# Drive products of the scan moved to GpSimd in the woven rows, with the first half's decays in PSUM

## The chip, the cores and the metric

One Trainium2 chip; the kernel runs on one core of it, in one launch. The metric is the device time of one execution in microseconds (us). The kernel before takes 1443.02 us (median of 3 runs, 1440.24 to 1448.51).

## What is computed

Four batch rows of 512 tokens with 128 channels pass four blocks, each followed by a residual sum and a layer norm: sparse latent attention, a mixture of 16 small experts, a Mamba layer, and a top-1 mixture of 8 experts. The change is in the Mamba layer, whose state recurrence is

```python
dA = jnp.exp(jnp.einsum('bld,dn->lbdn', delta, A))
dBu = jnp.einsum('bld,bln,bld->lbdn', delta, Bp, u)
def step(state, inp):
    a, b, c = inp
    state = a * state + b
    y = jnp.einsum('bdn,bn->bd', state, c)
    return (state, y)
```

with 256 inner channels d and 16 states n.

## The kernel before

Each batch row goes through `attention(b)` and then `rest(b)` (experts, Mamba layer, top-1 experts). The two are woven: while one row's attention runs, the row before goes through its rest. Every engine has its own queue of instructions, written by Python generators; a `yield` ends a phase, and `weave` takes one phase of the attention and then one of the rest, on each engine alike. What an engine has in its queue it executes in that order; between engines there are semaphores. So there are four rests: those of rows 0 and 1 stand in a hardware loop (`Fori`), whose semaphore thresholds are computed in registers, that of row 2 stands behind the loop with constant thresholds, woven too, and that of row 3 runs alone. Below they are the two loop rows, the third row and the last row.

The scan stage takes 16 steps, one for each state n; the 512 tokens lie on the free axis, 128 of the 256 channels on the partitions, and the two channel halves are j = 0 and 1. A step n consists of

- the decays, `exp(A_n * delta)`, 128x512 for each half, by ScalarE (ACT, L1201). In a woven row they go to SBUF (`dA`, a part of `big`, two buffers by n % 2), in the last row to PSUM banks 0 to 3;
- the drive product `dBu = DU * B_n`, 128x1024 for both halves, by VectorE (DVE, `drive`, L1713) in a woven row, by GpSimd (POOL, L1294) in the last row. It has two buffers as well;
- the two scans, `tensor_tensor_scan`, by VectorE (L1725);
- the readout product `hC = state * C_n` by VectorE (L1738, in the last row L1736), into XP and CV in turn;
- the sum over the states, by TensorE (PE, L866), in PSUM banks 5 and 6.

In a woven row VectorE issues the drive product of step n + 1 behind the scans of step n and ahead of its readout product, and the first one ahead of step 0. ScalarE issues the decays of steps 0 and 1 in the first phase and then, in each phase, those one step ahead. Rows B_n and C_n are spread over the partitions by DMAs of the SP queue, four steps ahead (tile `BC`). GpSimd has nothing to do in the woven scan stages.

Attention's instructions lie between the steps, among them one-hot builds of the picked key columns (VectorE, L1499, from float16 to bfloat16, SBUF to SBUF; TensorE L708 picks with them), copies of the picks (ScalarE L1068), top-k (MAX8, FIND_INDEX8, MATCH_REPLACE8), index scores (L1407, L1411), rotations (L1396), local maxima (L1460, with their negation `nml` L1465) and the spreading of the queries QBD (ScalarE L1052).

## Time and profile before

| | us |
|---|---|
| median of 3 runs | 1443.02 |
| the profiled execution | 1442.37 |
| its span, first to last instruction | 1440.6 |
| busy: TensorE (matmul) | 908.0 |
| busy: VectorE | 990.2 |
| busy: ScalarE | 584.6 |
| busy: GpSimd | 83.8 |
| scan stages of the loop rows, from the first scan | 107.4 each |
| scan stage of the third row | 102.5 |
| scan stage of the last row | about 60 |

The busy shares are means over stages with different limits; what a change is worth is read from the stage that it touches. In the rows below, a row of the instructions in order of time has the start, the duration, the engine, the line of the kernel, the operation, the tile written and those read, and the shapes; xN says how many instructions are merged in it. What stands in brackets is the engine's idle time in front and what ended it.

### The profile page before, as it was taken

What the parts mean: (1) busy time and instruction counts of PE and PEld (TensorE: products, weight loads), DVE (VectorE), ACT (ScalarE), POOL (GpSimd) and SP (SyncE); (2) the same over time, 40 slices, a digit from 0 to 9 for tenths busy, and PEclk for the clock granted to TensorE, in tenths of its full rate; (3) what the DMA queues carried; (4) which work ended last, traced back from release to release, by engine and by line L of the source; (5) the groups of instructions that cost most, each with busy time, mean ns of one, the idle gap of its engine ahead of it and who ended that gap; (6) DMA issues with size and microseconds to landing.
All of it is one profiled execution on the core that took longest, in us unless ns stands there. A gap on an engine that the chain in (4) does not pass through costs nothing.

```text
span 1440.6 us, 30987 instructions
## 1 busy us (share of the span) xinstructions
PE 908.0 (63%) x11808; PEld 541.5 (38%) x11808; DVE 990.2 (69%) x2294; ACT 584.6 (41%) x1278; POOL 83.8 (6%) x56
## 2 busy tenths in 40 slices
PE   4556656778456576677656568577757567562555
PEld 2334534445224253444323335344424235240122
DVE  4355553566799986655789986746789987344985
ACT  2423332566552332376544232366643331444320
POOL 0000000010000000011000000011000000030630
PEclk9566868597769789688769779598757879575895
DMA  4110110311232210221123310031033310302320
GB/s 140 30 39 10 32 39 10 68 35 35 70 82 76 57 31 18 51 50 38 62 62 79 82 30 7 13 88 39 15 92 96 79 34 10 67 0 60 110 66 8
DMA packets 84840, 72.38 MB, mean 50 GB/s; under 512 B 24528, under 2 KB 63440, under 8 KB 84496
## 3 DMA queue, kind: packets, MB, share of 16 engines
q1 hardware_dynamic: 84688, 70.34, 19.2%
q8 instruction: 97, 1.59, 0.5%
q14 instruction: 55, 0.45, 0.1%
HBM read 66.51 MB, written 3.80 MB: 49 GB/s over the span
## 4 chain that ended last, share of the span: by engine, by line
DVE 37%; PE 26%; issue 16%; ACT 13%; DMA 4%; SPq 3%; DVEq 1%; ACTq 0%; POOL 0%; POOLq 0%
DVE SG L1725 5%; PE bank L708 4%; PE bank L536 3%; DVE Y L1818 3%; PE bank L740 3%; SPq L473 2%; DVE XP L1738 2%; ACT relu_s L1016 2%; DVE CV L1738 2%; PE bank L866 2%; DVE bank L1725 1%; ACT QBD L1052 1%; DVE ml L1460 1%; PE bank L816 1%; DVE big L1700 1%
## 5 line engine op out<-in xcount | busy, mean ns | idle before, releaser
L708 PE MATMUL bank<-onehot,tparts 128*32 128x256 bf16 x3840 | 134.9, 300 | 46.0 <-DVE onehot L1499 45.1
L708 PEld LDWEIGHTS bank<-onehot,tparts 128*32 128x32 bf16 x3840 | 107.2, 105 | 82.6 <-DVE onehot L1499 44.4
L866 PE MATMUL bank<-XP,CO 128*128 128x512 f32 x128 | 84.6, 796 | 63.4 <-DVE XP L1736 33.8
L1725 DVE TENSOR_TENSOR_SCAN SG<-big 128x512 f32<-128x512 f32 x96 | 111.8, 1206 | 5.3 <-DVE score L1429 1.8
L1201 ACT ACTIVATE big<-DEL,Aneg 128x512 f32<-128x512 f32 x96 | 63.8, 715 | 109.1 <-DVE SG L1725 103.1
L1016 ACT ACTIVATE relu_s<-bank,nml 128x192 f32<-128x192 f32 (+1 forms) x128 | 53.0, 426 | 113.2 <-DVE nml L1465 113.2
L866 PE MATMUL bank<-CV,CO 128*128 128x512 f32 x128 | 74.1, 707 | 38.4 <-DVE CV L1738 26.3
L1499 DVE TENSOR_SCALAR onehot<-ib,CO 128x1024 bf16<-128x1024 f16 x160 | 69.8, 478 | 16.2 <-PE bank L708 11.0
L740 PE MATMUL bank<-GT,QBD 128*32 128x32 f32 x3072 | 55.8, 206 | 39.1 <-DVE G L1508 27.9
L1460 DVE TENSOR_REDUCE ml<-bank 128x2 f32<-128x384 f32 (+1 forms) x64 | 33.8, 569 | 67.1 <-PE bank L643 36.5
L536 PE MATMUL bank<-CO,relu_s 128*128 128x128 f32 (+2 forms) x256 | 46.2, 341 | 47.8 <-ACT relu_s L1016 47.8
L740 PEld LDWEIGHTS bank<-GT,QBD 128*32 128x32 f32 x3072 | 53.5, 117 | 46.2 <-issue 46.1
L1068 ACT ACTIVATE GT<-bank 128x256 f32<-128x256 f32 x64 | 24.5, 383 | 109.0 <-PE bank L708 108.8
L866 PEld LDWEIGHTS bank<-XP,CO 128*128 128x128 f32 x128 | 28.0, 242 | 102.8 <-issue 48.6
L1506 DVE TENSOR_TENSOR GT<-bank,rank_turn 128x512 f32<-128x512 f32 x64 | 44.0, 688 | 29.4 <-ACT GT L1068 28.7
L536 PEld LDWEIGHTS bank<-CO,relu_s 128*128 128x128 f32 (+2 forms) x256 | 36.4, 162 | 59.2 <-issue 57.7
L1713 DVE TENSOR_TENSOR big<-DU,BC 128x1024 f32<-128x1024 f32 x48 | 57.7, 1202 | 0.3
L1052 ACT ACTIVATE QBD<-QT 32x768 f32<-32x768 f32 x64 | 53.7, 839 | 7.3 <-DVE QT L1489 6.8
L816 PE MATMUL bank<-XRT,W 128*128 128x512 f32 (+1 forms) x72 | 52.7, 823 | 4.9 <-DVE U L1646 4.9
L536 PE MATMUL bank<-CO,QB 128*128 128x128 f32 x80 | 19.5, 391 | 56.2 <-DVE QB L1401 51.1
L866 PEld LDWEIGHTS bank<-CV,CO 128*128 128x128 f32 x128 | 25.0, 217 | 78.4 <-DVE CV L1738 36.9
L1818 DVE SCALAR_TENSOR_TENSOR Y<-bank,gate,Y 128x128 f32<-128x128 f32 x128 | 44.9, 351 | 13.1 <-PE bank L889 7.4
(313 smaller groups left out, 1999.4 us busy)
## 6 DMA issues: line engine op xcount, KB each, us to landing
BC<-bc_rows SPq DMA_DIRECT2D x128, 256.0 KB, 4.4
ib<-idx_rows SPq DMA_DIRECT2D x64, 256.0 KB, 4.1
big<-comb_rows SPq DMA_DIRECT2D x8, 1024.0 KB, 10.1
rows_bounce<-RO SPq DMA_DIRECT2D x256, 8.5 KB
W<-w SPq DMA_DIRECT2D x1, 2818.0 KB, 15.1
RB<-rows_bounce SPq DMA_DIRECT2D x16, 136.0 KB, 2.1
X<-x SPq DMA_DIRECT2D x4, 256.0 KB, 3.0
out<-CV SPq DMA_DIRECT2D x4, 256.0 KB, 2.3
```

Of the source, the lines that this page charges most:

```text
L536: return pe.transpose(o, i_, ident[0:k, 0:k])
L708: m = mm(bank[2 + c % 2][32 * bb:32 * bb + 32, 256 * kind:256 * kind + 256], tparts[:, kt, part, 32 * kind:32 * kind + 32], onehot[:, n % ...
L740: m = mm(bank[0][32 * a:32 * a + 32, 32 * xx:32 * xx + 32], QBD[:, kind, t, :, :].rearrange("p b h -> p (b h)"), GT[:, kind, t, :], start= ...
L816: mm(bank[k0][0:rows, :], wg, XRT[:, :], start=True, stop=True).then_inc(ga_ps.sem, ga_ps.up())
L866: mm(bank[5 + j][:, :], ident, hC[(n - 1) % 2][:, j, :], start=(n == 1), stop=(n == DS)).then_inc(ysum.sem, ysum.up())
L1016: m = A(PL[:, hh, c0:224], sc, ACT.Exp, scale=SCALE, bias=nml[:, h:h + 1], accum_out=ll[:, h:h + 1])
L1052: m = A(QBD[32 * bb:32 * bb + 32, :, :, bb, :], QT[32 * bb:32 * bb + 32, :, :, :], ACT.Copy)
L1201: A(decay, DEL[:, j, :], ACT.Exp, scale=Aneg[:, j, n:n + 1]).then_inc(dA_ok.sem, dA_ok.up())
L1499: TS(onehot[:, n % 4, :], ib[:, c, :], co("pos")[:, kt:kt + 1], None, ALU.is_equal).then_inc(oh_ok.sem, oh_ok.up())
L1713: TT(dBu[:, n % 2, :, :], DU[:, :, :], BC[:, n % ROWS_AHEAD, 0:1, :].to_broadcast([P, 2, L]), ALU.mult).then_inc(dBu_ok.sem, dBu_ok.up())
L1725: m = dve.tensor_tensor_scan(state, decay, dBu[:, n % 2, j, :], 0.0, ALU.mult, ALU.add)
L1818: STT(out=Y2[:, i, :], in0=bank[TOP1_BANKS[i][k]][:, e * P:(e + 1) * P], scalar=gate[:, i, 4 * k + e:4 * k + e + 1], in1=Y2[:, i, :], op0= ...
```

## The change

The drive products of the woven rows move from VectorE to GpSimd. GpSimd's product n waits for the readout of step n - 2 (in the last row, as before, for its scans). The decays of half j = 0 of a woven row go to PSUM bank 7, which has one buffer: ScalarE writes them after the first scan of the step before, for which the new signal `half_ok` stands, and issues j = 1 ahead of j = 0. ScalarE's decays of step n now stand in the phase of step n; they were one phase ahead.

```diff
--- before.py
+++ after.py
@@ -225,6 +225,13 @@
         ez, eu = big[:, 0, :, :], big[:, 1, :, :]
         BC = sb("BC", [P, ROWS_AHEAD, 2, L])
         hs = SG
+
+        def decay_of(n, j, alone):
+
+            if alone:
+                return bank[2 * (n % 2) + j][:, :]
+            return bank[7][:, :] if j == 0 else dA[:, n % 2, 1, :]
+
         last_states = (bank[4], bank[7])
         hC = (XP[:, :, DCONV - 1:], CV)
         YG = CV
@@ -364,6 +371,7 @@
         c_in = [signal(f"c_row_in_slot_{k}", DS // ROWS_AHEAD, 16) for k in range(ROWS_AHEAD)]
         dA_ok = signal("decay_ready", 2 * DS)
         dBu_ok = signal("drive_ready", DS)
+        half_ok = signal("first_half_states_ready", DS)
         scan_ok = signal("states_ready", DS)
         hC_ok = signal("readout_ready", DS)
         ysum = signal("readout_summed", 2 * DS)
@@ -1194,14 +1202,14 @@
                 yield
                 act.wait_ge(del_ok.sem, del_ok.at(b, 1))
                 for n in range(DS):
-                    for j in range(2):
+                    for j in (1, 0):
                         if n >= 2:
                             act.wait_ge(scan_ok.sem, scan_ok.at(b, n - 1))
-                        decay = bank[2 * (n % 2) + j][:, :] if alone else dA[:, n % 2, j, :]
-                        A(decay, DEL[:, j, :], ACT.Exp, scale=Aneg[:, j, n:n + 1]).then_inc(dA_ok.sem, dA_ok.up())
-                    if n >= 1:
-                        yield
-                for _ in range(4):
+                        if n >= 1 and j == 0 and not alone:
+                            act.wait_ge(half_ok.sem, half_ok.at(b, n))
+                        A(decay_of(n, j, alone), DEL[:, j, :], ACT.Exp, scale=Aneg[:, j, n:n + 1]).then_inc(dA_ok.sem, dA_ok.up())
+                    yield
+                for _ in range(3):
                     yield
                 norm_scale(b, 3)
                 yield
@@ -1285,15 +1293,17 @@
                 for _ in range(EXPERT_PHASES - 18 + NORM_PHASES + SCAN_IN_PHASES):
                     yield
                 for n in range(DS):
-                    if alone:
-                        pool.wait_ge(del_ok.sem, del_ok.at(b, 1))
-                        row_in = b_in[n % ROWS_AHEAD]
-                        pool.wait_ge(row_in.sem, row_in.at(b, n // ROWS_AHEAD + 1))
-                        if n >= 2:
-                            pool.wait_ge(scan_ok.sem, scan_ok.at(b, n - 1))
-                        pool.tensor_tensor(dBu[:, n % 2, :, :], DU[:, :, :], BC[:, n % ROWS_AHEAD, 0:1, :].to_broadcast([P, 2, L]),
-                                           ALU.mult).then_inc(dBu_ok.sem, dBu_ok.up())
-                    yield
+                    pool.wait_ge(del_ok.sem, del_ok.at(b, 1))
+                    row_in = b_in[n % ROWS_AHEAD]
+                    pool.wait_ge(row_in.sem, row_in.at(b, n // ROWS_AHEAD + 1))
+                    if n >= 2:
+                        free = scan_ok if alone else hC_ok
+                        pool.wait_ge(free.sem, free.at(b, n - 1))
+                    pool.tensor_tensor(dBu[:, n % 2, :, :], DU[:, :, :], BC[:, n % ROWS_AHEAD, 0:1, :].to_broadcast([P, 2, L]),
+                                       ALU.mult).then_inc(dBu_ok.sem, dBu_ok.up())
+                    if n >= 1:
+                        yield
+                yield
                 for _ in range(SCAN_OUT_PHASES + NORM_PHASES + TL1298 ISA [waits delta_ready]
L1302 TENSOR_TENSOR big<-DU,BC 128x1024 [waits b_row_in_slot_0]
L1298 ISA [waits delta_ready]
L1302 TENSOR_TENSOR big<-DU,BC 128x1024 [waits b_row_in_slot_1]
L1298 ISA [waits delta_ready]
L1301 ISA [waits b_row_in_slot_2]
L1302 TENSOR_TENSOR big<-DU,BC 128x1024 [waits readout_ready]
L1298 ISA [waits delta_ready]
L1301 ISA [waits b_row_in_slot_3]
L1302 TENSOR_TENSOR big<-DU,BC 128x1024 [waits readout_ready]1_PHASES):
                     yield
 
@@ -1707,25 +1717,15 @@
                 TT(DU[:, :, :], DEL[:, :, :], U[:, :, :], ALU.mult).then_inc(del_ok.sem, del_ok.up())
                 dve.wait_ge(del_ok.sem, del_ok.now(b))
 
-                def drive(n):
-                    row_in = b_in[n % ROWS_AHEAD]
-                    dve.wait_ge(row_in.sem, row_in.at(b, n // ROWS_AHEAD + 1))
-                    TT(dBu[:, n % 2, :, :], DU[:, :, :], BC[:, n % ROWS_AHEAD, 0:1, :].to_broadcast([P, 2, L]),
-                       ALU.mult).then_inc(dBu_ok.sem, dBu_ok.up())
-
-                if not alone:
-                    drive(0)
                 yield
                 for n in range(DS):
                     dve.wait_ge(dA_ok.sem, dA_ok.at(b, 2 * n + 2))
                     dve.wait_ge(dBu_ok.sem, dBu_ok.at(b, n + 1))
                     for j in range(2):
                         state = last_states[j][:, :] if alone else hs[:, j, :]
-                        decay = bank[2 * (n % 2) + j][:, :] if alone else dA[:, n % 2, j, :]
-                        m = dve.tensor_tensor_scan(state, decay, dBu[:, n % 2, j, :], 0.0, ALU.mult, ALU.add)
-                    m.then_inc(scan_ok.sem, scan_ok.up())
-                    if n < DS - 1 and not alone:
-                        drive(n + 1)
+                        done = (half_ok, scan_ok)[j]
+                        dve.tensor_tensor_scan(state, decay_of(n, j, alone), dBu[:, n % 2, j, :], 0.0, ALU.mult,
+                                               ALU.add).then_inc(done.sem, done.up())
                     dve.wait_ge(scan_ok.sem, scan_ok.now(b))
                     row_in = c_in[n % ROWS_AHEAD]
                     dve.wait_ge(row_in.sem, row_in.at(b, n // ROWS_AHEAD + 1))
```

In these pieces of the orders `waits` names the semaphores that an instruction waits for; rows marked ISA only wait or set registers, and a scan stands as SCALAR_TENSOR_TENSOR. VectorE, a loop row, steps 1 and 2 of the scan, the kernel before; `big` holds dBu and dA, SG the states, XP and CV the readout products:

```order
L1725 SCALAR_TENSOR_TENSOR SG<-big 128x512 [waits drive_ready]
L1725 SCALAR_TENSOR_TENSOR SG<-big 128x512
L1712 ISA
L1713 TENSOR_TENSOR big<-DU,BC 128x1024 [waits b_row_in_slot_2]
L1729 ISA
L1731 ISA [waits states_ready]
L1738 TENSOR_TENSOR CV<-SG,BC 128x1024 [waits c_row_in_slot_1]
L1740 ISA
L1720 ISA [waits readout_ready]
L1721 ISA [waits decay_ready]
```

and the same steps now:

```order
L1727 SCALAR_TENSOR_TENSOR SG<-bank7,big 128x512 [waits drive_ready]
L1727 SCALAR_TENSOR_TENSOR SG<-big 128x512
L1729 ISA
L1731 ISA [waits states_ready]
L1738 TENSOR_TENSOR CV<-SG,BC 128x1024 [waits c_row_in_slot_1]
L1740 ISA
L1722 ISA [waits readout_ready]
L1723 ISA [waits decay_ready]
L1727 SCALAR_TENSOR_TENSOR SG<-bank7,big 128x512 [waits drive_ready]
L1727 SCALAR_TENSOR_TENSOR SG<-big 128x512
```

The drive products have left VectorE's queue, and the first scan of each step reads bank 7. GpSimd, a loop row, had nothing behind the expert stage; now its queue goes on with these, steps 0 to 3:

```order
L1298 ISA [waits delta_ready]
L1302 TENSOR_TENSOR big<-DU,BC 128x1024 [waits b_row_in_slot_0]
L1298 ISA [waits delta_ready]
L1302 TENSOR_TENSOR big<-DU,BC 128x1024 [waits b_row_in_slot_1]
L1298 ISA [waits delta_ready]
L1301 ISA [waits b_row_in_slot_2]
L1302 TENSOR_TENSOR big<-DU,BC 128x1024 [waits readout_ready]
L1298 ISA [waits delta_ready]
L1301 ISA [waits b_row_in_slot_3]
L1302 TENSOR_TENSOR big<-DU,BC 128x1024 [waits readout_ready]
```

From step 2 on each waits for the readout of two steps before. ScalarE, a loop row, around the spreading of the queries (QBD), the kernel before; the decays after the two copies to `relu_s` are those of step 5:

```order
L1052 ACTIVATE QBD<-QT 32x96x8 [waits picked_scores_in_psum]
L1052 ACTIVATE QBD<-QT 32x96x8 x3
L982 ISA
L984 ISA [waits index_scores_in_psum]
L985 ACTIVATE relu_s<-bank0 128x448 [waits index_relu_used]
L982 ISA
L984 ISA [waits index_scores_in_psum]
L985 ACTIVATE relu_s<-bank1 128x448 [waits index_relu_used]
L1199 ISA
L1201 ACTIVATE big<-DEL,Aneg 128x512 [waits states_ready]
L1199 ISA
L1201 ACTIVATE big<-DEL,Aneg 128x512 [waits states_ready]
```

and now, where the pair after `relu_s` is that of step 4:

```order
L1060 ACTIVATE QBD<-QT 32x96x8 [waits picked_scores_in_psum]
L1060 ACTIVATE QBD<-QT 32x96x8 x3
L990 ISA
L992 ISA [waits index_scores_in_psum]
L993 ACTIVATE relu_s<-bank0 128x448 [waits index_relu_used]
L990 ISA
L992 ISA [waits index_scores_in_psum]
L993 ACTIVATE relu_s<-bank1 128x448 [waits index_relu_used]
L1207 ISA
L1210 ACTIVATE big<-DEL,Aneg 128x512 [waits states_ready]
L1207 ISA
L1209 ISA [waits states_ready]
L1210 ACTIVATE bank7<-DEL,Aneg 128x512 [waits first_half_states_ready]
```

The pair of decays has moved one step back against the attention's instructions, and its second half goes to bank 7 behind a wait for the first half's scan.

## Rows read from the trace of the kernel before

**Rows 1.** Scan stages: window, length, busy of PE, PEld, DVE, ACT, POOL; PEclk, DMA
```profile
743.90:851.30 107.40, 68.60 (x748) 34.98 (x749) 100.59 (x138) 34.87 (x74) 0.00 (x0) 0.78 0.30 72
1073.30:1175.80 102.50, 68.38 (x747) 34.81 (x748) 100.32 (x138) 34.35 (x72) 0.00 (x0) 0.77 0.30 75
```

**Rows 2.** VectorE in order of time, step 2 of the second loop row
```profile
753.59 2.34 DVE L1725 TENSOR_TENSOR_SCAN SG<-big 128x512 f32<-128x512 f32 x2 [0.25 <-DVE CV L1738]
755.85 1.20 DVE L1713 TENSOR_TENSOR big<-DU,BC 128x1024 f32<-128x1024 f32 x1
756.97 1.22 DVE L1738 TENSOR_TENSOR XP<-SG,BC 128x1024 f32<-128x1024 f32 x1
```

**Rows 3.** VectorE, last steps of the second loop row and of the third row
```profile
847.45 2.34 DVE L1725 TENSOR_TENSOR_SCAN SG<-big 128x512 f32<-128x512 f32 x2
850.04 1.23 DVE L1738 TENSOR_TENSOR CV<-SG,BC 128x1024 f32<-128x1024 f32 x1 [0.25 <-PE bank L866]
...
1172.23 2.34 DVE L1725 TENSOR_TENSOR_SCAN SG<-big 128x512 f32<-128x512 f32 x2
1174.61 1.23 DVE L1738 TENSOR_TENSOR CV<-SG,BC 128x1024 f32<-128x1024 f32 x1
```

**Rows 4.** GpSimd and VectorE in the last row's scan stage
```profile
1353.91 2.35 POOL L1294 TENSOR_TENSOR big<-DU,BC 128x1024 f32<-128x1024 f32 x1 [1.35 <-DVE bank L1725]
...
1355.10 2.35 DVE L1725 TENSOR_TENSOR_SCAN bank<-bank,big 128x512 f32<-128x512 f32 x2
...
1357.62 2.35 POOL L1294 TENSOR_TENSOR big<-DU,BC 128x1024 f32<-128x1024 f32 x1 [1.36 <-DVE bank L1725]
```

**Rows 5.** Both engines at once: last row's experts, first loop row; L1407 alone
```profile
1261.53 1.26 POOL L1282 TENSOR_TENSOR SZ<-SZ,big 128x512 f32<-128x512 f32 x1
...
1261.67 1.66 DVE L1635 TENSOR_TENSOR KI<-G,U 128x512 f32<-128x512 f32 x1 [9.68 <-POOL U L1282]
...
1263.86 0.68 DVE L1635 TENSOR_TENSOR XT<-GT,SZ 128x512 f32<-128x512 f32 x1
...
305.49 1.27 POOL L1282 TENSOR_TENSOR U<-U,big 128x512 f32<-128x512 f32 x1 [3.44 <-DVE U L1646]
...
306.19 0.68 DVE L1407 TENSOR_SCALAR score<-relu_s,W 128x192 f32<-128x192 f32 x1
...
74.78 0.28 DVE L1407 TENSOR_SCALAR score<-relu_s,W 128x192 f32<-128x192 f32 x1
```

**Rows 6.** A one-hot build ahead of a GpSimd product; MAX8 inside one
```profile
961.72 0.47 DVE L1499 TENSOR_SCALAR onehot<-ib,CO 128x1024 bf16<-128x1024 f16 x1
961.87 1.46 POOL L1282 TENSOR_TENSOR U<-U,big 128x512 f32<-128x512 f32 x1 [7.12 <-DVE U L1646]
...
313.60 1.27 POOL L1282 TENSOR_TENSOR SZ<-SZ,big 128x512 f32<-128x512 f32 x1 [6.84 <-DVE SZ L1646]
...
313.67 0.35 DVE L1424 MAX8 top<-score 128x8 f32<-128x192 f32 x1
```

**Rows 7.** Heads of steps 4, 8 and 13, second loop row; ScalarE's decays
```profile
764.62 1.28 DVE L1499 TENSOR_SCALAR onehot<-ib,CO 128x1024 bf16<-128x1024 f16 x3 [0.24 <-DVE CV L1738]
...
790.04 1.22 DVE L1738 TENSOR_TENSOR CV<-SG,BC 128x1024 f32<-128x1024 f32 x1
...
792.37 0.41 DVE L1407 TENSOR_SCALAR score<-relu_s,W 128x448 f32<-128x448 f32 x1
...
829.12 0.41 DVE L1396 TENSOR_TENSOR SRd<-SR,trig 128x256 f32<-128x256 f32 x1
...
764.54 1.35 ACT L1201 ACTIVATE big<-DEL,Aneg 128x512 f32<-128x512 f32 x2
```

**Rows 8.** VectorE at the head of the second loop row's scan stage
```profile
740.04 1.23 DVE L1713 TENSOR_TENSOR big<-DU,BC 128x1024 f32<-128x1024 f32 x1
...
742.97 0.17 DVE L1465 TENSOR_SCALAR nml<-ml 128x4 f32<-128x4 f32 x1
743.66 0.29 DVE L1389 TENSOR_TENSOR Y<-bank,Y 128x128 f32<-128x128 f32 x1 [0.52 <-PE bank L551]
```

## The prediction

> **What bounds the kernel now.** The change takes 48 drive products, 16 in each of three rows, from VectorE, at 1.20 us each [rows 2]. Whether those 57.6 us are time or cover is told by what I read first, the busy time of each engine in the scan stages. In the scan of a woven row VectorE is busy 100.6 of 107.4 us (loop rows) or 100.3 of 102.5 us (third row), TensorE 69, ScalarE 35, GpSimd 0 [rows 1]. So VectorE is the bound there, and the reader should see that each microsecond taken from it, or in which it is blocked, moves the end of the stage. Next I read VectorE's instructions in order of time, for what is hidden behind a drive product, and last every place of the trace where GpSimd and VectorE work at once.
>
> **What the removal saves.** In an ordinary step the two scans start at 753.59, the drive product of the next step at 755.85, the readout product at 756.97: 3.38 us from scans to readout [rows 2]. The last step of each row has no drive product behind its scans, so it is the changed step: 2.59 us in a loop row (847.45 to 850.04), 2.38 us in the third row (1172.23 to 1174.61) [rows 3]. The difference between the two is register arithmetic for the waits, which the loop rows pay after the scan has ended (the 0.25 us of idle in [rows 3]); the drive product covered it. A step therefore gains 3.38 - 2.59 = 0.79 us in the two loop rows and 1.00 us in the third, not 1.12. Fifteen steps a row: 11.9, 11.9 and 15.0 us. The sixteenth drive product, the one ahead of the first scan, gains nothing: behind it VectorE waits for TensorE anyway (the 0.52 us of idle and what lies before it, [rows 8]).
>
> **What GpSimd costs.** A drive product takes GpSimd 2.35 us [rows 4]; it has a whole step for it, now at least 3.38 + 1.22 + 0.25 = 4.85 us [rows 2], so the product itself is never late. The cost is what VectorE cannot do meanwhile. In the last row the scans read one operand in PSUM and run beside the drive product at full speed, two in 2.35 us [rows 4]. In the expert stage of that row a VectorE product with both operands in SBUF starts 0.14 us after a GpSimd product (1261.67 against 1261.53) and takes 1.66 us instead of 0.68: it ends 0.54 us after GpSimd does, so it stood still until GpSimd had finished. A TENSOR_SCALAR from SBUF to SBUF does the same: 0.68 us beside GpSimd, 0.28 without [rows 5]. In the other order GpSimd waits: with a one-hot build in flight it takes 1.46 us instead of 1.27 (as [rows 5] has it), while MAX8 runs inside a GpSimd product in its 0.35 us [rows 6]. So two kinds of VectorE instruction exclude GpSimd, those with two SBUF operands and those TENSOR_SCALARs; PSUM readers and one-operand instructions do not. A blocked one resumes as if it had started 0.15 us before GpSimd's end.
>
> The changed kernel moves the first half's decays to PSUM, so the first scan of a step is free; the second scan still has two SBUF operands. The Trainium skill ("SBUF — State Buffer", Who interferes with whom) says that a VectorE instruction with two SBUF inputs and a GpSimd one that reads SBUF take a shared port by an exclusive lock, whoever is first. By that rule the second scan is excluded as well, and the sum is the one below; by what the rows show and no more, it could be exempt, since none has a scan as the blocked one, and that is rival 3. I count it as excluded because it has the two SBUF operands of the product at 1261.67.
>
> GpSimd starts drive n+1 when readout n-1 is done, thus at the head of step n: 0.17 us after the readout in the loop rows (as the one at 1357.62 behind scans that ended at 1357.45 [rows 4]), and in the third an estimated 0.1 sooner, since no threshold is computed there. It lasts until 2.52 (2.42), and blocked work resumes at 2.37 (2.27). The stall of a step is that time less the time at which its first excluded instruction would have begun, per loop row:
> - Steps 1, 2, 9 have no attention work ahead of the scans. First scan at 0.25, second at 1.38: stall 0.99 each, 3.0.
> - Steps 4 to 7 begin with three one-hot builds at 0.24 [rows 7]: 2.13 each, 8.5. Half of the cost is here.
> - Step 8: the L1407 scaling stands 1.11 us behind the readout (792.37 against 790.04 + 1.22) [rows 7]: 1.26.
> - Step 13: the L1396 product stands 1.38 behind (829.12 against a readout's end at 827.74) [rows 7]: 0.99.
> - Step 14 begins with tiny products of two SBUF operands (L1359, L1361); the first gets in, the next, some 0.34 behind the readout, stands still: 2.0.
> - Steps 3, 10, 11, 12 begin with 1.7 to 3.4 us of transposes, MAX8 and PSUM readers: nothing. Step 15 has no drive product beside it.
> The sum is 15.8 us. In the third row VectorE goes on 0.03 us after a readout rather than 0.25: 3 x 1.13, 4 x 2.13 (the first one-hot build gets in, the second waits), 1.26, 1.10 and 2.0 make 16.3.
>
> At the head of the stage drives 0 and 1 follow each other on GpSimd: 4.65 us from the end of DU (about 739.9), to 744.7. The `nml` scaling, due at 742.97 [rows 8], is then blocked to 744.6, and scan 0 starts near 744.9 instead of 743.91: 1.0 us in the loop rows, in the third, by the same working with an earlier release, 0.6.
>
> **The decays.** ScalarE loses its one-step lead: in the order it now issues the pair of step n behind the attention work of the same step. The tightest place is step 4, where the pair stands behind QBD and two relu copies: ready at 764.54 + 1.35 = 765.89, while scan 4 follows the one-hot builds of 764.62 + 1.28 = 765.90 less overlap [rows 7]. With the builds 2.13 late this costs nothing; without a stall it would cost about 0.9 us a row. The pair's second member, into bank 7, waits for the first scan of the step before, which ends more than 2.5 us before it is wanted: nothing.
>
> **Sum.** Loop rows: -11.9 + 15.8 + 1.0 = +4.9 each. Third row: -15.0 + 16.3 + 0.6 = +1.9. Together +11.7 us. The last row's stream changes only in the order of two exponentials: 0. The profiled execution took 1442.4 us (span 1440.6), so 1454.1; the median of the runs shown is 1443.0, 0.6 above. I forecast 1454.
>
> Bounds of the terms. The saving can be 0.79 to 1.12 a step (the whole distance from drive to readout): 38.8 to 50 us. The stalls reach from 0 (nothing is blocked) to 64 us (2.13 in each of the 3 x 10 steps that have one); I take 47.9 + 2.6, nearer to the upper end because the rows that show both engines at excluded instructions, [rows 5], show a full stop each time.
>
> **Rivals.**
> 1. *VectorE keeps its turn through a run of one-hot builds.* Nothing in the trace shows three excluded instructions in a row with GpSimd waiting. If GpSimd gets in only behind the third (1.5 us), it runs beside the PSUM readers and the first scan, and the stall is 0.9 in step 4 and 0.15 in 5 to 7: 1.35 instead of 8.5 a row, -21.5 in all, 1433. Against it: in the loop rows GpSimd's start comes 0.07 us before the first build's. The point from which it decides is whether GpSimd or the queued build goes on at the first one's end.
> 2. *No exclusion that matters.* The plain reading of the busy shares: VectorE is the bound and loses work. -38.8 us, and 0.9 x 3 back for late decays in step 4: 1406. For it: 92% of the stage's time on VectorE. Against it: the two blocked rows of [rows 5].
> 3. *Scans are never blocked.* The stalls of steps 1, 2 and 9 go, 3.0 + 3.0 + 3.4 = 9.3 us: 1445, no change. For it: no row shows a blocked scan. Against it: the product at 1261.67 [rows 5] has the same kinds of operands.
> 4. *The decays come late as well.* ScalarE's pair, 1.34 us, is exposed in a dozen of the 48 steps: +16 beside the stalls, 1470. For it: the zero margin of step 4. Against it: GpSimd's stalls delay VectorE by more than ScalarE's queue is late, and elsewhere the margin is over 2 us.
>
> **How the numbers follow.** Forecast 0.60, with its own range of 1448 to 1463; rival 1 0.12, rival 2 0.06, rival 3 0.12, rival 4 0.10. A measurement of this kernel can tell about 0.5%, 7.2 us: faster is below 1435.8, slower above 1450.2. Of the forecast 0.06 lies under 1450.2. Slower: 0.54 + 0.10 = 0.64; same: 0.06 + 0.12 = 0.18; faster: 0.12 + 0.06 = 0.18. The range from 1432 to 1466 takes in rivals 1 and 3, and leaves out rival 2 and most of rival 4.
>
> **What would show it.** The scan stages of the loop rows should last 111 to 112.5 us (107.4 before) and that of the third row 104 to 105 (102.5), with VectorE's busy time hardly lower, since a blocked instruction counts as busy: fewer instructions with longer means. The first one-hot build of steps 4 to 7 should show some 2.6 us instead of 0.48, the second scans of steps 1, 2 and 9 some 2.2 instead of 1.20, `nml` at the head some 1.8. Scans to readout should be 2.59 and 2.38 us in unblocked steps. One-hot builds at 0.48 throughout would prove rival 1 (GpSimd's products then take over 3 us) or rival 2 (GpSimd's at 2.35); VectorE idle ahead of scans with ScalarE as releaser would prove rival 4. I am wrong if the stages get shorter.

## The result, and the profile after

The changed kernel takes 1456.57 us (median of 14 runs, 1448.41 to 1462.39), the kernel before 1440.46 us (median of 14 runs, 1436.49 to 1448.51). The ratio is 1.0101, with a 95% interval of 1.0078 to 1.0123: 1.0% slower, 14.5 us (11 to 18). The means of the runs lie 14.5 us apart, the medians 16.1. The forecast was 1454 us, 11.7 us over the profiled execution of before.

In the diff under "The change", ten rows of an order stand inside one line of GpSimd's part; the line reads `for _ in range(SCAN_OUT_PHASES + NORM_PHASES + TOP1_PHASES):` and is the same in both kernels.

The busy time by engine in the scan stages, from the first scan to the end of the last readout product, second loop row and third row; the columns are those of [rows 1]. First the kernel before, in windows cut the same way:

```profile
743.91:851.27 107.36, 68.57 (x748) 34.95 (x749) 100.58 (x138) 34.86 (x74) 0.00 (x0) 0.78 0.30 72
1073.27:1175.84 102.57, 68.42 (x748) 34.85 (x749) 100.38 (x138) 34.38 (x72) 0.00 (x0) 0.77 0.30 75
```

and now:

```profile
752.49:863.17 110.68, 69.43 (x748) 34.47 (x749) 100.02 (x123) 36.09 (x76) 32.89 (x14) 0.78 0.27 70
1088.87:1193.30 104.43, 68.81 (x742) 33.84 (x743) 101.73 (x123) 36.15 (x76) 33.76 (x14) 0.78 0.27 74
```

VectorE has lost 15 instructions of 1.20 us, 18 us of work, and its busy time has moved by only -0.6 and +1.4 us; the stages are 3.3 and 1.9 us longer. A blocked instruction counts as busy, so the busy share hides the loss: the count of instructions tells it. The page's groups show where the time went; of a group the last columns are busy us, mean ns, idle before:

```profile
L1302 POOL TENSOR_TENSOR big<-DU,BC 128x1024 f32<-128x1024 f32 x64 | 151.1, 2363 | 448.6 <-DVE DU L1717 243.6
...
L1509 DVE TENSOR_SCALAR onehot<-ib,CO 128x1024 bf16<-128x1024 f16 x160 | 93.8, 628 | 23.5 <-PE bank L716 18.8
...
L1727 DVE TENSOR_TENSOR_SCAN SG<-big 128x512 f32<-128x512 f32 x48 | 66.6, 1387 | 0.0
...
L1727 DVE TENSOR_TENSOR_SCAN SG<-bank,big 128x512 f32<-128x512 f32 x48 | 58.1, 1209 | 5.3 <-DVE score L1439 1.2
```

The scans whose decays lie in PSUM (`SG<-bank,big`) kept their 1.21 us; those with both operands in SBUF went from 1.20 to 1.39 on average; the one-hot builds went from 69.8 us in all to 93.8. In order of time, step 1 of the second loop row, VectorE and then GpSimd:

```profile
754.95 1.23 DVE L1738 TENSOR_TENSOR XP<-SG,BC 128x1024 f32<-128x1024 f32 x1
756.43 1.22 DVE L1727 TENSOR_TENSOR_SCAN SG<-bank,big 128x512 f32<-128x512 f32 x1 [0.25 <-DVE XP L1738]
757.57 2.12 DVE L1727 TENSOR_TENSOR_SCAN SG<-big 128x512 f32<-128x512 f32 x1
759.83 1.22 DVE L1738 TENSOR_TENSOR CV<-SG,BC 128x1024 f32<-128x1024 f32 x1
```

```profile
756.26 2.35 POOL L1302 TENSOR_TENSOR big<-DU,BC 128x1024 f32<-128x1024 f32 x1 [3.91 <-DVE XP L1738]
```

GpSimd starts 0.08 us after the readout product has ended at 756.18. The first scan runs beside it undisturbed, the second takes 2.12 us instead of 1.20: it ends 1.08 us after GpSimd, the product in [rows 5] ended 0.54 us after it, each its own length less some 0.13 (1.20 - 1.08 and 0.68 - 0.54). The head of step 4, to be set beside [rows 7]:

```profile
771.71 3.25 DVE L1509 TENSOR_SCALAR onehot<-ib,CO 128x1024 bf16<-128x1024 f16 x3 [0.24 <-DVE CV L1738]
774.88 1.21 DVE L1727 TENSOR_TENSOR_SCAN SG<-bank,big 128x512 f32<-128x512 f32 x1
```

```profile
771.54 2.35 POOL L1302 TENSOR_TENSOR big<-DU,BC 128x1024 f32<-128x1024 f32 x1 [3.06 <-DVE CV L1738]
```

Three builds took 1.28 us before and take 3.25: 1.97 lost. In the third row VectorE is first and still loses; the last of these rows has the shortest, the median and the longest of the three builds in ns:

```profile
1107.21 3.38 DVE L1509 TENSOR_SCALAR onehot<-ib,CO 128x1024 bf16<-128x1024 f16 x3
...
L1509 DVE TENSOR_SCALAR onehot<-ib,CO x3: 475/487/2580, 1107.2 to 1110.1; 128x1024 bf16<-128x1024 f16 x3
```

```profile
1107.34 2.56 POOL L1302 TENSOR_TENSOR big<-DU,BC 128x1024 f32<-128x1024 f32 x1 [2.64 <-DVE CV L1738]
```

GpSimd waits for the end of the first build (2.56 us instead of 2.35), then it goes ahead of the second, which takes 2.58 us instead of 0.48. And the head of the stage, where [rows 8] had `nml` at 0.17 us:

```profile
749.92 1.02 DVE L1470 TENSOR_REDUCE ml<-bank 128x2 f32<-128x384 f32 x2 [2.40 <-PE bank L651]
750.98 1.39 DVE L1475 TENSOR_SCALAR nml<-ml 128x4 f32<-128x4 f32 x1
752.29 0.28 DVE L1399 TENSOR_TENSOR Y<-bank,Y 128x128 f32<-128x128 f32 x1
```

### The profile page after: what moved, and what is told of

It reads as the page before. It is cut to its first block, busy times and chain, and to the rows that moved or that the text cites. A ratio compares the mean times of both kernels' runs of the same rounds, so it can differ in the third digit from the quotient of the medians.

```text
span 1454.8 us, 31075 instructions
## 1 busy us (share of the span) xinstructions
PE 916.1 (63%) x11808; PEld 545.7 (38%) x11808; DVE 991.1 (68%) x2246; ACT 584.4 (40%) x1278; POOL 197.2 (14%) x104
## 4 chain that ended last, share of the span: by engine, by line
DVE 29%; PE 28%; issue 22%; ACT 11%; DMA 4%; SPq 4%; POOL 1%; DVEq 1%; ACTq 0%; POOLq 0%
PE bank L716 6%; PE bank L544 3%; SPq L481 3%; PE bank L748 3%; DVE SG L1727 2%; DVE Y L1818 2%; ACT relu_s L1024 2%; PE bank L874 2%; PE bank L897 2%; DVE bank L1727 1%; DVE ml L1470 1%; DVE onehot L1509 1%; PE bank L824 1%; DMA RB<-rows_bounce 1%; DVE big L1710 1%
## 5 line engine op out<-in xcount | busy, mean ns | idle before, releaser
L1302 POOL TENSOR_TENSOR big<-DU,BC 128x1024 f32<-128x1024 f32 x64 | 151.1, 2363 | 448.6 <-DVE DU L1717 243.6
L716 PE MATMUL bank<-onehot,tparts 128*32 128x256 bf16 x3840 | 141.8, 311 | 56.4 <-DVE onehot L1509 56.1
L1509 DVE TENSOR_SCALAR onehot<-ib,CO 128x1024 bf16<-128x1024 f16 x160 | 93.8, 628 | 23.5 <-PE bank L716 18.8
L874 PE MATMUL bank<-CV,CO 128*128 128x512 f32 x128 | 77.9, 739 | 39.2 <-DVE CV L1738 27.1
L1210 ACT ACTIVATE bank<-DEL,Aneg 128x512 f32<-128x512 f32 x80 | 53.7, 684 | 118.5 <-DVE SG L1727 74.0
L1727 DVE TENSOR_TENSOR_SCAN SG<-big 128x512 f32<-128x512 f32 x48 | 66.6, 1387 | 0.0
L1290 POOL TENSOR_TENSOR U<-U,big 128x512 f32<-128x512 f32 x20 | 27.2, 1362 | 281.5 <-DMA big<-comb_rows 193.4
L1727 DVE TENSOR_TENSOR_SCAN SG<-bank,big 128x512 f32<-128x512 f32 x48 | 58.1, 1209 | 5.3 <-DVE score L1439 1.2
```

Of the source, the lines that this page charges most:

```text
L716: m = mm(bank[2 + c % 2][32 * bb:32 * bb + 32, 256 * kind:256 * kind + 256], tparts[:, kt, part, 32 * kind:32 * kind + 32], onehot[:, n % ...
L874: mm(bank[5 + j][:, :], ident, hC[(n - 1) % 2][:, j, :], start=(n == 1), stop=(n == DS)).then_inc(ysum.sem, ysum.up())
L1210: A(decay_of(n, j, alone), DEL[:, j, :], ACT.Exp, scale=Aneg[:, j, n:n + 1]).then_inc(dA_ok.sem, dA_ok.up())
L1302: pool.tensor_tensor(dBu[:, n % 2, :, :], DU[:, :, :], BC[:, n % ROWS_AHEAD, 0:1, :].to_broadcast([P, 2, L]), ALU.mult).then_inc(dBu_ok.se ...
L1509: TS(onehot[:, n % 4, :], ib[:, c, :], co("pos")[:, kt:kt + 1], None, ALU.is_equal).then_inc(oh_ok.sem, oh_ok.up())
L1727: dve.tensor_tensor_scan(state, decay_of(n, j, alone), dBu[:, n % 2, j, :], 0.0, ALU.mult, ALU.add).then_inc(done.sem, done.up())
```

## The experiments

The theory: while GpSimd works on a product, VectorE cannot run a product or a scan with two SBUF operands nor a TENSOR_SCALAR between SBUF tiles; the time follows from where each drive product starts and how long it lasts. Rivals: the decays, one phase later on ScalarE and half of them in a single PSUM bank, cost the time; or GpSimd's product costs the same wherever it stands.

The table has, for each kernel, the ratio to the kernel before and the time from the end of `DU` to the end of the last readout product in the three woven rows (worked out from starts and durations in order of time). Those lengths repeat within 0.3 us between the two loop rows in all kernels, so they tell more than the whole time, whose interval reaches 3 to 6 us to either side.

| kernel | median us | ratio, 95% interval | loop rows, third row |
|---|---|---|---|
| before | 1440.5 to 1444.6 | | 111.4, 111.4, 107.0 |
| changed | 1456.6 | 1.0101, 1.0078 to 1.0123 | 115.7, 115.7, 109.3 |
| drives back on VectorE | 1442.1 | 0.9998, 0.9974 to 1.0021 | 111.4, 111.4, 106.1 |
| GpSimd: half width | 1421.9 | 0.9869, 0.9831 to 0.9907 | 104.5, 104.4, 97.1 |
| GpSimd: 16 of 512 tokens | 1406.6 | 0.9748, 0.9710 to 0.9787 | 100.7, 100.7, 92.7 |
| GpSimd: drives 4, 11, 12, 13 | 1434.7 | 0.9960, 0.9933 to 0.9988 | 109.5, 109.2, 103.5 |
| before, GpSimd: drives 11, 12, 13 | 1436.1 | 0.9932, 0.9902 to 0.9962 | 109.0, 109.0, 104.5 |
| drives 6, 7, 8 too, behind the builds | 1431.2 | 0.9912, 0.9876 to 0.9949 | 107.8, 107.9, 102.2 |
| released at the scans | 1473.5 | 1.0208, 1.0165 to 1.0251 | 129.1, 129.1, 107.1 |
| whole and half drives by the rule | 1418.1 | 0.9811, 0.9779 to 0.9844 | 104.1, 104.1, 97.9 |

### Drives back on VectorE, everything else as changed

```diff
+        ON_POOL = ()
...
+                    if alone or n in ON_POOL:
...
+                if not alone and 0 not in ON_POOL:
+                    drive(0)
...
+                    if n < DS - 1 and not alone and n + 1 not in ON_POOL:
+                        drive(n + 1)
```

> The drive products go back to VectorE; the decays in bank 7, their order and their phase on ScalarE stay as changed. My theory (VectorE stands still while a GpSimd product runs) expects all stalls gone and the gain gone with them: within 2 us of the kernel before, about 1442; second scans of steps 1, 2 and 9 back at 1.20 us, one-hot builds at 0.48. The rival (the decays, one phase later, cost the time) expects the loss to stay: 1450 to 1457, with VectorE idle ahead of scans behind ScalarE.

Measured: ratio 0.9998, the loop rows as before, the third row 0.9 us shorter. The late decays show at one place, scan 4. In the kernel before it starts 0.09 us before the end of the three builds, in this one 0.09 us after it (step 4 of the second loop row, first the kernel before):

```profile
764.62 1.28 DVE L1499 TENSOR_SCALAR onehot<-ib,CO 128x1024 bf16<-128x1024 f16 x3 [0.24 <-DVE CV L1738]
765.81 2.33 DVE L1725 TENSOR_TENSOR_SCAN SG<-big 128x512 f32<-128x512 f32 x2
...
764.00 1.28 DVE L1511 TENSOR_SCALAR onehot<-ib,CO 128x1024 bf16<-128x1024 f16 x3 [0.24 <-DVE CV L1750]
765.37 1.22 DVE L1737 TENSOR_TENSOR_SCAN SG<-bank,big 128x512 f32<-128x512 f32 x1
```

So decays in bank 7, their order and their later phase cost 0.2 us a row as long as the drive products stay on VectorE, and a scan that reads PSUM costs nothing: the rival of the late decays falls. At the head of the third row's stage the new order even gains. ScalarE has two decays and not four ahead of the copy to `OT`, which TensorE's L551 waits for; the copy starts 1.3 us behind the end of `DU` instead of 2.5, and scan 0 3.4 us behind it instead of 4.4. The prediction did not have this gain. In the third row, the kernel before and then this one:

```profile
1071.39 0.36 ACT L1039 ACTIVATE OT<-bank 128x256 f32<-128x256 f32 x1
...
1069.15 0.36 ACT L1048 ACTIVATE OT<-bank 128x256 f32<-128x256 f32 x1
```

(`DU` ends at 1068.88 and 1067.87.) What is left as the cause of the loss is GpSimd's product.

### GpSimd's instruction at half the width

```diff
-                    pool.tensor_tensor(dBu[:, n % 2, :, :], DU[:, :, :], ...
+                    some = slice(0, 2 if alone else 1)
+                    pool.tensor_tensor(dBu[:, n % 2, some, :], DU[:, some, :], ...
```

> In the woven rows GpSimd multiplies only the first channel half (the second half's drive product is left out), so that its instruction takes some 1.27 us instead of 2.35. If VectorE stands still for as long as GpSimd's instruction runs, each stall shrinks by 1.08 us: the stalls of steps 1, 2, 9 and 13 vanish, those of 4 to 7 and 14 halve to 1.0. Per loop row -11.9 + 5.4 = -6.5 us, third row -9.5 us, together 22 us under the kernel before: about 1420. If the decays or something else make the time, nothing changes against the changed kernel: 1456.

Half of the drive products is left out here, so the kernel computes something else and only its time is read. Measured 1421.9, ratio 0.9869 (20 us by the medians, 24 in the stages); loop rows -7.0 us, third row -9.9. VectorE waits for as long as GpSimd's instruction lasts. Step 1 of the second loop row, where the product is over before the second scan, and its GpSimd product:

```profile
739.87 1.22 DVE L1728 TENSOR_TENSOR_SCAN SG<-bank,big 128x512 f32<-128x512 f32 x1 [0.25 <-DVE XP L1739]
741.01 1.20 DVE L1728 TENSOR_TENSOR_SCAN SG<-big 128x512 f32<-128x512 f32 x1
```

```profile
739.70 1.27 POOL L1303 TENSOR_TENSOR big<-DU,BC 128x512 f32<-128x512 f32 x1 [4.91 <-DVE XP L1739]
```

The builds of step 4:

```profile
753.30 2.17 DVE L1510 TENSOR_SCALAR onehot<-ib,CO 128x1024 bf16<-128x1024 f16 x3 [0.24 <-DVE CV L1739]
```

They lose 0.89 us instead of 1.97: the difference, 1.08, is that of the two products' lengths (2.35 - 1.27). In the third row, where GpSimd starts 0.1 us later, the second scans of steps 1, 2 and 9 still lose 0.14 us each (1.34 instead of 1.20).

### GpSimd's instruction next to nothing

```diff
+                    cols = L if alone else 16
+                    pool.tensor_tensor(dBu[:, n % 2, :, 0:cols], DU[:, :, 0:cols], ...
```

> In the woven rows GpSimd multiplies only 16 of the 512 tokens of each half (the rest of the drive product is left out); order, waits and signals are those of the changed kernel. It shows what the change would bring if GpSimd's products stopped nobody: -11.9 us in each loop row, -15.0 in the third, and at most 3 us back for decays that come late in step 4: about 1406, 36 us under the kernel before. If the decays' lost lead costs more than that, VectorE's idle time ahead of scans shows it and the time stays above 1412.

Most of the drive products is left out, so again only the time is read. Measured 1406.6. This is the gain that the change would bring if GpSimd disturbed nobody: 36 us in place of the loss, and all of it lies in the three stages (10.7 + 10.7 + 14.3). In the stages the changed kernel is 46.6 us longer than this one (15.0 + 15.0 + 16.7). Its trace shows 14.9 + 14.9 + 16.8 us of stalls, and each of its three heads is 1.06 us longer than here, 49.8 us; this kernel in turn waits 3.1 us for late decays. 49.8 - 3.1 = 46.7: the stalls account for the difference in the stages. By the medians the two kernels are 50 us apart, so some 3 us lie outside. The late decays show here once in each row:

```profile
751.56 1.28 DVE L1510 TENSOR_SCALAR onehot<-ib,CO 128x1024 bf16<-128x1024 f16 x3 [0.24 <-DVE CV L1739]
753.71 1.22 DVE L1728 TENSOR_TENSOR_SCAN SG<-bank,big 128x512 f32<-128x512 f32 x1 [0.87 <-ACT bank L1210]
```

Scan 4 waits 0.87 us for ScalarE, in the third row 1.09. In the kernel before it had no idle time in front and started 0.09 us ahead of the builds' end, as shown above, so the wait costs 0.96 us in a loop row and 1.18 in the third. The forecast had 0.9 a row.

### Only the drives that fall on free heads

```diff
+        ON_POOL = (4, 11, 12, 13)
...
+                    if alone or n in ON_POOL:
```

with the others back in VectorE's queue.

> GpSimd makes only drives 4, 11, 12 and 13 in the woven rows, which run at the heads of steps 3, 10, 11 and 12, where VectorE has 1.7 to 3.4 us of work that GpSimd does not stop; the others are on VectorE, as in the kernel before. My theory expects the full gain of four products and no stall: 4 x 0.79 in each loop row, 4 x 1.00 in the third, less up to 0.8 a row where step 4 then waits for its decays: 8 to 10 us under the kernel before, about 1434. If the stalls did not depend on what VectorE does meanwhile, four products would cost as in the changed kernel, 4/15 of +14: about +4 us.

Measured 0.9960: 5.8 us faster than the kernel before (1.7 to 9.7; 7.6 in the stages), less than the 8 to 10 expected. Nothing is stopped, as the theory has it, but two things eat into the gain. Drive 4 brings 0.79 us and scan 4 then comes 0.96 us late for its decays (idle 0.87, as above); in the third row it is 1.00 against 1.18. So drive 4 is a loss of 0.2 us a row; the 0.8 a row that I had set against it at most was too low. And in the loop rows the readout product of step 10 has 0.60 us of idle in front instead of 0.25:

```profile
811.73 1.23 DVE L1750 TENSOR_TENSOR XP<-SG,BC 128x1024 f32<-128x1024 f32 x1 [0.60 <-DVE SG L1737]
```

That takes 0.35 of drive 11's 0.79 us; its cause is open (see the sum below). Drives 12 and 13, and in the third row drive 11, bring their full gain.

### The kernel before with three of its drives moved

```diff
+        ON_POOL = (11, 12, 13)
...
-                    if alone:
+                    if alone or n in ON_POOL:
...
-                            pool.wait_ge(scan_ok.sem, scan_ok.at(b, n - 1))
+                            free = scan_ok if alone else hC_ok
+                            pool.wait_ge(free.sem, free.at(b, n - 1))
...
-                    if n < DS - 1 and not alone:
+                    if n < DS - 1 and not alone and n + 1 not in ON_POOL:
```

> The kernel before with one edit: GpSimd makes drives 11, 12 and 13 of the woven rows, released by the readout of two steps before; bank 7 is not used, both decays stay in SBUF and one phase ahead. At the heads of steps 10 to 12 VectorE has 2.2 to 3.4 us of work that GpSimd does not stop, so the PSUM decays should not be needed: 3 x 0.79 in each loop row and 3 x 1.00 in the third, 7.7 us under the kernel before, about 1434.5. If a scan with both operands in SBUF is stopped there all the same, the gain is nil.

Measured 0.9932: 9.8 us less (5.5 to 14.2; 7.2 in the stages), loop rows -2.34 us each (3 x 0.78), third row -2.5. With three products its stages gain nearly what those of the kernel above gain with four (7.2 and 7.6 us). Both decays are in SBUF; in the loop rows the product is over before the scans. In the third row the one ahead of step 12 is not, and its first scan takes 1.37 us instead of 1.22; 0.35 us of idle without a known cause in step 11 is the other part that is missing from 3 x 1.00. VectorE at the head of step 10, and the product:

```profile
800.59 1.22 DVE L1740 TENSOR_TENSOR CV<-SG,BC 128x1024 f32<-128x1024 f32 x1
802.05 0.43 DVE L1531 TENSOR_REDUCE RO<-bank 128x8 f32<-128x256 f32 x1 [0.24 <-DVE CV L1740]
802.51 0.42 DVE L1533 TENSOR_TENSOR SRd<-bank,RO 128x256 f32<-128x256 f32 x1
802.85 0.62 DVE L1426 MAX8 top<-score 128x8 f32<-128x448 f32 x1
...
805.25 2.34 DVE L1727 TENSOR_TENSOR_SCAN SG<-big 128x512 f32<-128x512 f32 x2 [0.36 <-DVE score L1431]
```

```profile
801.89 2.35 POOL L1296 TENSOR_TENSOR big<-DU,BC 128x1024 f32<-128x1024 f32 x1 [128.70 <-DVE CV L1740]
```

Each of them has the duration that it has without GpSimd, though GpSimd works from 801.89 to 804.24.

### Drives 6, 7 and 8 too, started behind the one-hot builds

```diff
+        ON_POOL = (4, 6, 7, 8, 11, 12, 13)
...
+                        if not alone and n in (6, 7, 8):
+                            built = round_of(2, n - 4, 0)
+                            pool.wait_ge(oh_ok.sem, oh_ok.at(row_after(b), built))
```

> As the run with four products on GpSimd, and drives 6, 7 and 8 too, but these start only when the one-hot builds at the heads of steps 5, 6 and 7 have ended, so that they run beside PSUM readers and the first scan. My theory (only the place of the product counts): the builds stay at 0.48 us, the second scans of steps 5 to 7 lose some 0.26, each such product gains 0.5 in a loop row and 0.7 in the third: together 13 us under the kernel before, 1429. If a product costs VectorE its 2.1 us wherever it starts, 12 us more: 1441.

Measured 0.9912, 12.7 us (11.8 in the stages). The same three products that cost 1.97 us each at the heads of steps 5 to 7 now cost 0.35 (0.43 in the third row, 2.10 before):

```profile
766.23 1.28 DVE L1514 TENSOR_SCALAR onehot<-ib,CO 128x1024 bf16<-128x1024 f16 x3 [0.24 <-DVE XP L1753]
767.42 0.68 DVE L1521 TENSOR_TENSOR GT<-bank,rank_turn 128x512 f32<-128x512 f32 x1
768.02 0.44 DVE L1523 STREAM_TRANSPOSE G<-bank 128x256 f32<-128x256 f32 x1
768.39 1.18 DVE L1740 TENSOR_TENSOR_SCAN SG<-bank,big 128x512 f32<-128x512 f32 x1
769.50 1.55 DVE L1740 TENSOR_TENSOR_SCAN SG<-big 128x512 f32<-128x512 f32 x1
```

```profile
767.59 2.37 POOL L1307 TENSOR_TENSOR big<-DU,BC 128x1024 f32<-128x1024 f32 x1 [11.58 <-DVE onehot L1514]
```

So the place of the product decides, and not that it is there.

### Released by the scans instead of the readout

```diff
-                        free = scan_ok if alone else hC_ok
+                        free = scan_ok
```

> The changed kernel, with GpSimd's products released by the second scan of two steps before instead of its readout. In the loop rows GpSimd then starts 0.08 us behind the scan and the readout product, due at 0.25, stands still for 2.0 us in each of 14 steps: -11.9 + 28.4 = +16.5 a row; in the third row the readout product starts first and GpSimd waits, so that the row costs as in the changed kernel, +2. Together some 36 us over the kernel before, about 1478, and 20 over the changed one. If only the length of GpSimd's products counted and not who starts first, it would stay at 1456.

Measured 1473.5, ratio 1.0208: 30 us over the kernel before (24 to 36), where 36 were expected; the stages alone are 17.7, 17.7 and 0.2 us longer, together 35.6, at the edge of that interval. In the loop rows the readout product is the victim in each of steps 0 to 13; it takes 3.36 us instead of 1.22 in step 1 and 2.9 to 3.4 in all:

```profile
766.38 1.20 DVE L1727 TENSOR_TENSOR_SCAN SG<-big 128x512 f32<-128x512 f32 x1
767.72 3.36 DVE L1738 TENSOR_TENSOR CV<-SG,BC 128x1024 f32<-128x1024 f32 x1
```

```profile
767.66 2.34 POOL L1302 TENSOR_TENSOR big<-DU,BC 128x1024 f32<-128x1024 f32 x1 [3.75 <-DVE SG L1727]
```

GpSimd starts 0.06 us ahead. In the third row VectorE goes on 0.03 us behind its scans and the readout gets in first. GpSimd waits for it, its product ends 2.2 us behind the readout (2.5 to 2.7 in the changed kernel), and so the same instructions are blocked as there (the builds of step 4 take 3.24 us), while the readout products keep their 1.23. The row is 0.2 us longer than before where a loop row is 17.7 us longer, and 3.1 us of that difference is the third row's larger saving (15.0 against 11.9): the rest shows that who starts first decides.

### Whole and half drives, each where it disturbs nobody

```diff
+        ON_POOL = (4, 6, 7, 8, 11, 12, 13)
+        HALF_ON_POOL = (2, 3, 5, 9, 10, 14, 15)
...
+                        if not alone and n == 15:
+                            pool.wait_ge(dm_ok.sem, dm_ok.at(row_after(b), 3))
+                        if not alone and n in HALF_ON_POOL:
+                            pool.tensor_tensor(dBu[:, n % 2, 1, :], DU[:, 1, :], BC[:, n % ROWS_AHEAD, 0, :],
+                                               ALU.mult).then_inc(dBu2_ok.sem, dBu2_ok.up())
...
+                decay(0, 1)
+                for n in range(DS):
+                    decay(n, 0)
+                    if n + 1 < DS:
+                        decay(n + 1, 1)
+                    yield
```

> A version built from the stall rule. GpSimd makes the whole drives 4, 11, 12, 13 and, behind the one-hot builds, 6, 7, 8; of drives 2, 3, 5, 9, 10, 14 and 15 it makes the second channel half alone (some 1.27 us, drive 5 behind the builds, 15 behind the max gaps), VectorE the first half; drives 0 and 1 are on VectorE. The decays of half 1 are issued one step ahead again, which takes away the wait of step 4 (0.62 and 1.06 us where GpSimd made drive 4). Expected: 8.4 us in each loop row and 9.4 in the third, 26 under the kernel before, about 1416. If the halves are stopped or stop VectorE more than that, it ends near the gated version, 1429.

In a part of the diff that is not shown, drives 5 to 8 wait for the builds as in the kernel above, and VectorE makes half 0 of the halved drives. Measured 1418.1, ratio 0.9811 (0.9779 to 0.9844): 27 us faster than the kernel before, and some 40 faster than the changed one (38 by the two medians, 42 by the two ratios). Step 1 of the second loop row, VectorE and GpSimd:

```profile
741.49 1.22 DVE L1759 TENSOR_TENSOR_SCAN SG<-bank,big 128x512 f32<-128x512 f32 x1 [0.25 <-DVE XP L1772]
742.63 1.20 DVE L1759 TENSOR_TENSOR_SCAN SG<-big 128x512 f32<-128x512 f32 x1
743.75 0.67 DVE L1742 TENSOR_TENSOR big<-DU,BC 128x512 f32<-128x512 f32 x1
744.33 1.22 DVE L1772 TENSOR_TENSOR CV<-SG,BC 128x1024 f32<-128x1024 f32 x1
```

```profile
741.32 1.26 POOL L1317 TENSOR_TENSOR big<-DU,BC 128x512 f32<-128x512 f32 x1 [73.20 <-DVE XP L1772]
```

The half product fits between the readout and the second scan, and VectorE's own half still covers the 0.25 us between scans and readout. In the third row the half product does not quite fit: the second scans of steps 1, 2 and 9 take 1.34 us. With half 1's decays one step ahead, scan 4 still waits for bank 7, but less: it starts 0.34 us later behind the readout than in the kernel before in a loop row (0.57 in the third) instead of 0.96 (1.18).

## Why the prediction was right, step by step

**The bound.** VectorE's time was the stage's time: taking 15 products away with no disturbance (the tiny product) shortened the loop rows by 10.7 us and the third by 14.3, and blocked time lengthened them one for one. The 10.7 us are the saving of 11.9 less 0.96 for late decays and 0.35 for the pause in step 11, and the small gains at the head; the third row's are 15.0 less 1.18, with 0.57 gained at the head.

**The saving.** Forecast 0.79 us a step in a loop row (from [rows 3]) and 1.00 in the third. Measured from scans to readout: 2.59 and 2.36 to 2.38 us, as forecast; in steps 0 and 1 of the loop rows 2.48. In steps 3 to 7 it is less, but so it was before (3.33 became 2.54), and the gain is the same.

**The stalls, per loop row.** Steps 1, 2, 9: forecast 0.99, measured 0.92 (the second scan 2.12 instead of 1.20). Steps 4 to 7: 2.13, measured 1.97 to 1.99. Step 8: 1.26, measured 1.16. Step 13: 0.99, measured 0.92. Step 14: 2.0, measured 2.1, where not the second but the first tiny product was blocked (in the third row it was the second). The sum is 14.9 instead of 15.8. In the third row it is 16.8 instead of 16.3, with 1.22 where 1.13 was forecast for the second scans and 2.10 for 2.13 at the builds. I had the starts of GpSimd the wrong way round, 0.17 us after the readout in the loop rows and 0.07 in the third: it was 0.08 and 0.17. That moved each term by a tenth and no conclusion.

**The head.** `nml` was blocked as forecast, until GpSimd's second product ended, and that end sets scan 0: it stood 0.96 us later behind DU in the loop rows (forecast 1.0) and 0.5 in the third (0.6). `nml` itself took 1.39 us in the second loop row and not 1.8, since its turn came later: TensorE's L643 in front of it (L651 now) took 1.64 us instead of 1.25.

**The decays.** No wait at step 4 in the changed kernel, since the one-hot builds are later still; 0.96 us in a loop row and 1.18 in the third once the stall is gone (forecast about 0.9).

**The sum.** Forecast +4.9, +4.9 and +1.9; measured from the end of DU +4.3, +4.3 and +2.4: 11.0 us in place of 11.7. In a loop row that is -11.9 + 14.9 + 0.96 and 0.35 us of idle before the readout product of step 11. I have no cause for this 0.35; it stands there with the tiny product too (0.60 us of idle instead of 0.25), so the length of GpSimd's product does not make it, and it is at step 10 with four products on GpSimd. Counted from the first scan, a loop row's stage is 110.7 us, just under the 111 to 112.5 that the prediction named as its sign, and the third row's is 104.4, within 104 to 105. What the stages do not account for is the rest of the 14.5 us, 3.5 us with an uncertainty of 3 of its own. The kernels run the same instructions up to the first scan stage, yet the ten profiled executions end their first DU between 404.6 us (the kernel before) and 410.3 us (the changed one), so single executions wander by as much outside the stages. It stays open whether anything beyond the stages is the change's. That the median of 1456.6 lies only 2.5 us from the forecast 1454.1 is in part luck: by the medians 5.1 us lie outside the stages, where nothing was forecast, while the kernel before came out 1.9 us under the 1442.4 from which the forecast started, and the stages 0.7 under theirs.

**The rivals.** Rival 1 (VectorE keeps its turn through a run of builds) is refuted by the third row: GpSimd waited for one build and went ahead of the second. Rival 2 (nothing is blocked) gave 1406 as its time, which is what the kernel with GpSimd's tiny product takes, but the premise is false. (The argument for it, 92% of the stage's time on VectorE, should read 94%: 100.6 of 107.4 us.) Rival 3 (scans are never blocked) falls with the 2.12 us scans. No row of before had a blocked scan; the forecast rested on the product at 1261.67, which has the same kinds of operands. The Trainium skill's rule ("SBUF — State Buffer", Who interferes with whom), by which a VectorE instruction with two SBUF inputs contends with a GpSimd one that reads SBUF, says the same, and the trace agrees (2.12 us instead of 1.20). Rival 4 (late decays) is refuted by the run with the drives on VectorE, and in the woven rows of the changed kernel no scan waits for ScalarE.

## What to carry to other kernels

Before work goes from VectorE to an idle GpSimd, list what VectorE runs in the window of each moved instruction: on this kernel the same product costs nothing beside PSUM readers, MAX8 and transposes, and up to 2.1 us beside a product or scan with two SBUF operands or an SBUF-to-SBUF TENSOR_SCALAR. Choose the semaphore that starts it accordingly, and cut it to the length of the free window; moving seven drives wholly and seven by half by that rule, with half of the decays issued one step ahead again, turned +1.0% into -1.9%. Look also at what else the change delays: drive 4 was free of stalls and still a loss, because its decays came late. And judge by instruction counts and mean durations, since blocked time reads as busy time.

## What the runs showed of the hardware that I had not expected

A waiting GpSimd instruction is served between two queued VectorE instructions: with three one-hot builds in a row it went in behind the first (2.56 us instead of 2.35 for the product, 2.58 instead of 0.48 for the second build, as shown for the third row). And a vector product whose operands and result are 8 elements wide in each partition waits as long as any other. Step 14 of the second loop row:

```profile
847.27 2.32 DVE L1369 TENSOR_TENSOR mj<-ml,RB 128x8 f32<-128x8 f32 x1
849.62 0.17 DVE L1371 TENSOR_TENSOR dm<-ml,mj 128x8 f32<-128x8 f32 x1
```

The next, of the same size, takes 0.17 us with GpSimd done.
